# Four attention walks over edges: the next chunk's softmax chain is started a quarter of a chunk earlier, on three engines

## The reference

```python
h = jnp.einsum('nf,fhd->nhd', x, W)
a_src = jnp.sum(h * att_src, axis=-1)
a_dst = jnp.sum(h * att_dst, axis=-1)
e = jax.nn.leaky_relu(a_src[src] + a_dst[dst], NEG_SLOPE)
e_max = jax.ops.segment_max(e, dst, num_segments=N)
e_exp = jnp.exp(e - e_max[dst])
denom = jax.ops.segment_sum(e_exp, dst, num_segments=N)
alpha = e_exp / (denom[dst] + 1e-16)
msg = h[src] * alpha[:, :, None]
out = jax.ops.segment_sum(msg, dst, num_segments=N)
```

## Time and profile before

| | us |
|---|---|
| median of 3 runs | 6823.27 (6819.3 to 6825.32) |
| the profiled execution | 6820.69 |
| its span in the trace | 6818.9 |

### The profile page before, as it was taken

One profiled execution on the slowest core, in us unless ns is written; L12 is line 12 of the kernel. 1 busy time (PEld: TensorE's weight loads), 2 busy tenths in 40 slices (PEclk: granted clock), 3 DMA queues, 4 the chain that ended last, 5 costly groups with the idle time before them and its releaser, 6 DMA issues. The chain is left out here.

```text
span 6818.9 us, 79751 instructions
## 1 busy us (share of the span) xinstructions
PE 4848.6 (71%) x19231; PEld 3393.1 (50%) x19232; DVE 3942.6 (58%) x8585; ACT 2371.9 (35%) x5719; POOL 3022.1 (44%) x2932
## 2 busy tenths in 40 slices
PE   2777659537775937776577738888899555477999
PEld 2455436325553725544355534444587333355777
DVE  4566733446667246665466657666424788787333
ACT  1343312124443224443244424544221122275333
POOL 2666432446662046662666536666000677553000
PEclk8777859767887968887688858888899665687999
DMA  4455424234442034443444511111001899873000
GB/s 117 151 167 166 106 66 127 86 103 143 152 153 61 1 105 152 143 152 90 144 142 152 133 41 29 31 31 26 21 9 51 315 379 381 295 220 118 10 14 23
DMA packets 543457, 819.09 MB, mean 120 GB/s; under 512 B 87966, under 2 KB 421967, under 8 KB 542839
## 3 DMA queue, kind: packets, MB, share of 16 engines
q1 hardware_dynamic: 396388, 432.93, 19.6%
q0 software_dynamic: 140832, 376.78, 19.3%
q10 hardware_dynamic: 5907, 5.92, 0.3%
HBM read 658.06 MB, written 157.71 MB: 120 GB/s over the span
## 5 line engine op out<-in xcount | busy, mean ns | idle before, releaser
L780 POOL DMA_INDIRECT l_edges_stage<-l_h_rows,src_t x832 | 822.6, 989 | 592.7 <-issue 222.5
L2507 POOL DMA_INDIRECT l_edge_kv<-l_kv_rows,src_t x416 | 477.0, 1147 | 651.1 <-POOLq L2414 517.5
L1093 PE MATMUL l_edges_ps_sum<-l_edges_msg,l_edges_hot 128*128 128x264 f32 x1664 | 591.0, 499 | 213.4 <-DVE l_attn_acc L922 134.1
L2935 POOL DMA_INDIRECT l_gate_edges_srow<-l_gate_src_rows,l_gate_edges_idx x512 | 487.1, 951 | 325.7 <-issue 140.8
L2560 PE MATMUL l_edge_ps_q<-l_q_q,l_edge_hot 128*128 x832 | 352.5, 598 | 287.6 <-issue 201.7
L3071 PE MATMUL l_gate_edges_ps<-l_gate_edges_wide,l_gate_edges_hot_lo 128*128 128x500 f32 x1024 | 492.8, 627 | 83.3 <-issue 57.3
L780 POOL DMA_INDIRECT l2a_edges_stage<-l2a_h_rows,src_t x416 | 408.2, 981 | 295.6 <-issue 126.5
L1093 PEld LDWEIGHTS l_edges_ps_sum<-l_edges_msg,l_edges_hot 128*128 128x128 f32 x1664 | 357.6, 239 | 362.9 <-DVE l_attn_acc L922 207.8
L780 POOL DMA_INDIRECT l2b_edges_stage<-l2b_h_rows,src_t x416 | 408.6, 982 | 288.6 <-issue 126.2
L2560 PEld LDWEIGHTS l_edge_ps_q<-l_q_q,l_edge_hot 128*128 128x128 f32 x832 | 238.4, 300 | 401.8 <-issue 353.9
L922 DVE TENSOR_TENSOR l_attn_acc<-l_attn_acc,l_edges_ps_sum 128x264 f32 x832 | 349.8, 420 | 84.5 <-DVE l_attn_acc L922 20.3
(11 more groups left out here) (784 smaller groups left out, 10870.1 us busy)
## 6 DMA issues: line engine op xcount, KB each, us to landing
l_edge_e<-e_rows SPq DMA_DIRECT2D x416, 128.0 KB
l_val_rows<-l_edge_vj SPq DMA_DIRECT2D x104, 512.0 KB
l_agg_stage<-l_val_rows SPq DMA_DIRECT2D x52, 1024.0 KB, 5.5
l_edges_rel_b<-rel_rows SPq DMA_DIRECT2D x52, 512.0 KB
l_edges_ea<-in_edge_attr SPq DMA_DIRECT2D x48, 512.0 KB
e_rows<-l_edges_e_s SPq DMA_DIRECT2D x48, 512.0 KB
l_experts_w<-in_L_ffn_w SPq DMA_DIRECT2D x32, 512.0 KB, 5.0
l_gate_edges_lo_b<-l_gate_edges_lo_rows SPq DMA_DIRECT2D x64, 256.0 KB
```

The costliest lines, as they stand in the source:

```text
L780: nc.gpsimd.indirect_dma_start(out=stage[:, c % SL, u, :], out_offset=None, in_=h_rows, in_offset=bass.IndirectOffsetOnAxis(ap=K.src_t[:, ...
L1093: nc.tensor.matmul(ps_sum[u][:], hot[:, g, u, :], msg[:, g % 2, u, :], start=True, stop=True).then_inc(summed, 1)
L2507: nc.gpsimd.indirect_dma_start(out=kv[:, m, u, :], out_offset=None, in_=kv_rows, in_offset=bass.IndirectOffsetOnAxis(ap=K.src_t[:, n * EB ...
L2935: nc.gpsimd.indirect_dma_start(out=srow[:, n % 4, u, :], out_offset=None, in_=src_rows, in_offset=bass.IndirectOffsetOnAxis(ap=idx[:, n * ...
```

## The change

Nothing is added or removed: the same instructions run in another order on DVE, PE and ACT. POOL and SP keep their streams and their waits as they are.

- DVE: `rescale` and `logits` of chunk c+1 now come ahead of the first `weigh` of chunk c. `tile_ends` follows that weigh directly, with no adds woven in; `tile_tops` carries the adds of group 0 (before: of group 1), `edge_maxima` those of group 1 (before: 2). Weigh 3 and the adds of groups 2 and 3 follow.
- PE: `turn_logits` comes ahead of scatter 0; `place_ends`, `place_tops`, then `place_f` with `turn_maxima`, each move ahead by one scatter; the last scatter is no longer split. The side job keeps its places between the scatters: the first `turn_attr` between 0 and 1, its product between 1 and 2, the second `turn_attr` between 2 and 3.
- ACT: `rescaling` moves from behind group 3 to behind group 1.

```diff
--- before.py
+++ after.py
@@ -924,24 +924,29 @@
                     return add
 
                 def chunk(c, j, i, after):
-                    weigh(c, i, 0)
                     blks = block_ids(nc, mybir.EngineType.DVE, K, c)
                     rescale(c, blks[0])
                     if after >= 1:
                         logits(c + 1, j, i + 1)
-                    for g, step in enumerate((tile_ends, tile_tops, edge_maxima)):
+                    weigh(c, i, 0)
+                    if after >= 1:
+                        tile_ends(c + 1, i + 1, lambda u: None)
+                    for g, step in ((0, tile_tops), (1, edge_maxima)):
                         weigh(c, i, g + 1)
                         if after >= 1:
                             step(c + 1, i + 1, adds(c, g, blks))
                         else:
                             for u in range(GR):
                                 adds(c, g, blks)(u)
+                    weigh(c, i, 3)
+                    for u in range(GR):
+                        adds(c, 2, blks)(u)
                     if after >= 1:
                         exponents(c + 1, i + 1)
                     if after >= 2:
                         nodes_hot(c + 2, j, i + 2)
                     for u in range(GR):
-                        adds(c, GR - 1, blks)(u)
+                        adds(c, 3, blks)(u)
 
                 if zr is not None:
                     zr.clear(dve)
@@ -1003,10 +1008,11 @@
                             keep_turned(c, 0)
                         edges_hot(c, g)
                         last_maxima(c, m, g)
+                        if after and g == 1:
+                            rescaling(c + 1, 1 - m)
                     if j is not None:
                         keep_terms(c, m, 0, j * 16 + 16)
                     if after:
-                        rescaling(c + 1, 1 - m)
                         edges_hot(c + 1, 0)
                         if j is not None:
                             keep_turned(c, 1)
@@ -1093,29 +1099,27 @@
                         nc.tensor.matmul(ps_sum[u][:], hot[:, g, u, :], msg[:, g % 2, u, :], start=True, stop=True).then_inc(summed, 1)
 
                 def chunk(c, m, after, j=None):
+                    if after >= 1:
+                        turn_logits(c + 1, 1 - m)
                     scatter(c, 0)
                     if after >= 1:
-                        turn_logits(c + 1, 1 - m)
+                        place_ends(c + 1)
                     if after >= 2:
                         turn_attr(c, m, 0, j * 16 + 16 * (m + 1))
                     scatter(c, 1)
                     if after >= 1:
-                        place_ends(c + 1)
+                        place_tops(c + 1)
                     if after >= 2:
                         attr_terms(c, 0)
                     scatter(c, 2)
                     if after >= 1:
-                        place_tops(c + 1)
+                        place_f(c + 1)
+                        turn_maxima(c + 1)
                     if after >= 2:
                         turn_attr(c, m, 1, None)
-                    scatter(c, 3, 0, GR // 2)
-                    if after >= 1:
-                        place_f(c + 1)
-                        turn_maxima(c + 1)
-                    scatter(c, 3, GR // 2)
+                    scatter(c, 3)
                     if after >= 2:
                         blks = block_ids(nc, mybir.EngineType.PE, K, c + 2)
-                    if after >= 2:
                         attr_terms(c, 1)
                         expand(c + 2, m, blks)
```

## The result

The changed kernel takes 7249.55 us (median of 4 runs, 7243.1 to 7271.48) against 6824.3 in the same series (6819.3 to 6827.51): a ratio of 1.0628, with a 95% interval of 1.0612 to 1.0644. The profiled execution has a span of 7250.6 us. It is slower by 425 us, as forecast in sign; the forecast was 7125 with a range of 6900 to 7340.

The account below looks back on a forecast made before the run. A chain between DVE and PE, with PE's signals held during POOL's gather runs, was taken to bound the kernel; 14.0 + 12.3 + 2.8 = 29.1 us a chunk against 25.84, over 92 chunks, gave 7125 us, range 6900 to 7340.

Parts of the forecast that it names:

- The kernel is bound by a chain of stages, and PE's signals are held deep in a run: PE's signals during POOL's gathers are seen only when the run stops, some 2.4 us after its last gather's start.
- the lag is PE's own: Rival: `inits_made` is seen 3.3 us behind `place_tops` whatever POOL does; about 27.0 us a chunk, 6930 us; chance 0.11.
- Stage A: From `msg_built` of group 0 to `inits_made` seen: ten gathers, `place_tops` seen only when the run stops; 14.0 us.
- Stage B: From DVE's copy of `inits_made` to the end of `expand`: 12.3 us, between 10.5 and 15.5.
- `place_tops` gets through: Rival: POOL does not stop after ten gathers but runs 14, stopping for `max_turned`; 29.5 us a chunk, 7160 us; chance 0.10.
- Stage C: From the end of `expand` to POOL's next start: reduce, logits and weigh follow each other; 2.8 us.
- The sum: A whole chunk: 14.0 + 12.3 + 2.8 = 29.1 us against 25.84, 3.3 more over 92 chunks.
- The loop's turn: Every sixth chunk, DVE's 4.83 us stand ahead of the weigh falls into the wait for a late `expand`.
- PE's clock: PE's slowing after its longer stand was left open, with bounds of 6957 and 7420 us on the time.
- that sign: In the changed trace, PE's mean clock in the walks would be lower; no size given.
- its case of the whole stage at the lower level: PE's longer stand keeps its work from the `inits_made` copy through `expand` at 1.2 GHz: 15.5 us, about 7420 us.

Follow-up runs that it names:

- b_free_pool: The kernel before without POOL's four waits in mid-group; 7394.41 us, ratio 1.083.
- b_own_gathers: The kernel before with POOL's four mid-group waits replaced, at the same places, by waits for its own gathers to have landed; 7288.29 us, ratio 1.0682.
- a_stop_early: The changed kernel with POOL's waits for `inits_made` and `max_turned` moved to the start of their groups; 7052.47 us, ratio 1.0334.
- run 16: Not a follow-up run: the words are "a run 16% were", the share of PE's signals seen late during the first two gathers of a run of gathers.
- b_head_only: The kernel before with only DVE's new head: block load, rescale and logits ahead of weigh 0; 7076.54 us, ratio 1.0373.

## Why the prediction was right, and where not

**The kernel is bound by a chain of stages, and PE's signals are held deep in a run.** Right for the first three series: `b_free_pool` (8.8 us in nine chunks instead of 3.0), `b_own_gathers` (54.2 to 1.9 us) and `a_stop_early` (197 us for two moved waits) bear it out. The trace of before, counted over its four walks, shows how it grows with the run. Of the signals that PE gave with no gather under way none of 354 was seen late; during the first two gathers of a run 16% were, during the third and fourth 32%, the fifth to eighth 77%, and behind that 97%. So there is no sharp point at the fifth or sixth gather, where the prediction put one, and the third is not always early enough. Not right for the other two series, in which neither the holds nor, for the old order, the chain as the bound are there. The rival "the lag is PE's own" is out by the same runs, and by the traces without holds. The Trainium skill (SBUF — State Buffer, Who interferes with whom) says that a DMA never contends with a compute engine. It says so of the ports of SBUF, and no run here tests those; the prediction read it as a rule for signals too, and read so, the last two series agree with it and the first three do not.

**Stage A, 14.0 us.** 14.07 in the chunk shown, with ten gathers, `place_tops` 8.4 us in and in the seventh gather, as forecast. A little of the hit is luck: the gathers follow each other at 1.26 us and not 1.286, and the copy comes 2.73 us behind the last gather's start and not 2.46. And it isn't so in all chunks. In 6 of the 21 chunks of the first walk the signal is seen 11.3 to 12.8 us after POOL's start, before the run stops (the copy at 326.50 for one). It is late even so, by 3.2 to 4.6 us, but POOL goes on without a stop, and stage B is 15 to 18 us instead of 10. This is near the rival "`place_tops` gets through", and it takes turns with the forecast within one walk. The two don't cost the same, as that rival's price (29.5 against 29.1) said: from one `expand` to the next the six chunks take 33.4 us on average (30.8 to 36.0), the other fifteen 29.3 (26.7 to 32.8).

**Stage B, 12.3 us.** 10.0 in the chunk shown, 10.3 on average in the fifteen chunks that go as forecast, 15.8 in the six others, and over the first walk, both kinds together, about 12. The working put 12.3 together from the scatters; for the chunks that it describes it is 2 us too much.

**Stage C, 2.8 us.** This is the term that was mis-sized: 5.6 us in the chunk shown, 4.9 on average in the fifteen. The prediction let reduce, logits and weigh follow `expand` directly. It had the load of the block numbers in its order rows and gave it no time, because before it lay under the first weigh and took 1.10 us. Without that cover it takes 2.87 in the median and up to 3.40. In the chunk shown the DMA engines were 94% busy behind `expand`; whether that makes the load longer wasn't tested. From the end of `expand` to the reduce it makes 2.6 us in the median chunk. Moving it away made the chunks of the forecast's kind 1.9 us shorter, but there were fewer of them, and only 61 us came back.

**The sum, 29.1 us a chunk.** In the fifteen chunks of the forecast's kind it came out at 29.3, and that is luck: stage B was 2 us shorter than forecast and stage C 2 us longer. The 30.66 us of the whole walk are more mainly because of the six chunks of the other kind, 4 us longer each. (92 x 3.3 is 304 and not 302, which changes nothing.)

**The loop's turn, absorbed.** Wrong in two of three. Before, DVE stood 4.83 us there. In the first walk of the changed kernel stage C is 8.7 and 9.3 us long at the first and the third turn, and at the second, where `expand` came late, 5.1. In the other chunks it is at most 5.6. The turn isn't covered, since the turn comes ahead of the load and the rescale, and `expand` isn't late enough to cover both.

**PE's clock.** The bounds were right and the upper one not reached: scatter 0 behind the stand runs at 0.52, the end of stage B at 1.00. The mean clock in the first walk is nearly the same as before (0.77 and 0.78 by the windows), so that sign hardly came.
The Trainium skill (TensorE: Matmul & The Clock Gate, Part 1), by which only activity releases the throttled clock, agrees with scatter 0 after PE's 0.48 us of work in 5.54, and its case of the whole stage at the lower level did not come.

**What the forecast had too simple.** It gave stage A as the main loss. With no hold at all the new order, with POOL's stops moved, still loses 5.5%, nearly all of it through stage B, against an old order that is then bound by POOL's gathers. With the holds the kernel before pays 3.0 us at L879 and the changed one 5.1. Of the 425 us, 197 hang on the places of two of POOL's stops; the rest is not parted between the order and the holds.

## What to carry to other kernels

When a link is moved ahead of a piece of work, price what that piece had covered: here a weigh and a register load lay under the wait for `expand`, and laid bare they cost 251 us on their own (`b_head_only`); the engine that had stood came back at half clock (0.52) for its next scatter. A wait in a queue of gathers can be worth more than the gathers lose by it: taking four away cost 8%, moving two by two gathers gave 2.7% back. A stage forecast should be compared chunk by chunk and not by the mean: here two kinds of chunk took turns. And test a cause on more than one chip before it becomes a rule: the hold that explained every row of one chip was absent on the next.

## What the runs showed of the hardware

- In three series PE's signals were seen late deep in a run of indirect DMAs (419.34 seen at 425.05; in the trace of before none late outside of runs, 77% late during the fifth to eighth gather), DVE standing up to 9.7 us for one where nothing stopped POOL; in two others, on other chips, they were not, even in runs of 416 gathers, and the kernel before ran in 6173 to 6180 us instead of 6825.
- A load of 16 numbers into DVE's registers takes 1.10 us, and in the changed kernel 2.87 in the median and up to 3.40; the DMA engines were 94% busy in the stretch of one of 3.40.
- A stop of POOL for its own last gather costs 3.0 us on average.
- POOL issues an indirect gather each 1.26 us when nothing stops it; 416 of them set the length of a walk in the last two series (523 to 526 us in three of the four).
